# Transposes of the attention weights woven between the projections, values two phases behind their scores, attention weights in two buffers

## The chip, the cores and the metric

The kernel runs on one core of one Trainium2 chip. The metric is the device time in microseconds. TensorE (PE) multiplies matrices and writes PSUM, VectorE (DVE), ScalarE (ACT) and GpSimd (POOL) do the rest, SyncE (SP) issues the DMA transfers. PEld is TensorE's weight load, which has rows of its own.

## What is computed

128 graphs of 128 nodes, model width 512, 16 heads of width 32. All tensors are float32.

```python
q, k, v = (split_heads(x @ W.T) for W in (Wq, Wk, Wv))
a = einsum('bhnd,bhmd->bhnm', q, k) * scale + (adj + adj)[:, None]
a = where(any(a != 0, axis=-1, keepdims=True), a, -inf)
p = softmax(a); p = where(isnan(p), 0, p)
o = merge_heads(einsum('bhnm,bhmd->bhnd', p, v)) @ Wo.T
return layernorm(x + o)
```

## The kernel before, in words

A group is GG = 4 graphs (512 rows of x); there are 32 groups. A group has TILES = 4 phases, one for each four heads, so there are PHASES = 128 phases, numbered f = 4g + t. One phase handles four graphs times four heads, that is 16 score matrices of 128x128.

A projection (kinds k, q, v, o) is one 128x512 product with a contraction over 512. To keep float32 accuracy with the fp32r type, both operands are split in a high and a low part (`split_product`, L334): for each of the four chunks two matmuls (L338 with the low, L339 with the high part crossed) and then four of high times high (L341), 12 matmuls of 128x512 in one PSUM bank. An output of kind k, q or v is copied out of its bank by ACT (`take`, L454), one of kind o is added to x by DVE (`add`, L587), which then takes the statistics for the layernorm; POOL works out the scale and shift (`ln`, L284) and ACT applies them (`normalise`, L486); SP stores.

One phase on PE (L428 to L447) is, in this order:

- `turn(f-1)`, L388: 16 transposes of the last phase's attention weights `e_sb` (128x128 each), four (a quad, one graph) to one bank; ACT copies each quad to `e_t` (`turned_out`, L504).
- `scores(f)`, L397: 16 products, one for each graph and head, that use 32 rows of the array each (the trace has 32 records of them) into four banks `ps_s`.
- `values(f-1)`, L411: the product of `e_t` and v, again 16 products and 32 records, 32 columns of the array each, into `ps_o`. ACT takes the high part (`values_hi`), DVE the low part (`values_lo`).
- the projections of `slots(f)`, four in an inner phase by `PLAN` (L37): k and q for the next head tile, and two of kind v (for the next group) or o (for the last group).

Projections and quads share the BANKS = 3 banks `ps_w` in the order of `bank_uses()` (L72): use u takes bank u mod 3, and `wait_bank(u)` (L344) makes PE wait until use u-3 has been copied out (`k_copied`, `q_copied`, `v_copied`, `turned_copied`, or `added` for o).

DVE's phase: `add` of the last phase's last o, `values_lo(f-2)`, doubling of the adjacency once a group, `bias(f)` (L606, score plus bias and its row minimum, 16 instructions), `any_nonzero` (L621), then in two halves reciprocals (L637) and `normalise` (L645, which multiplies `e_sb`), then `add` of the third slot. ACT's phase: the last copy, the four quads, layernorm, the four `exps(f, i)` (L495, 4 activations each) with the copies of the first two slots among them, `values_hi(f-1)`, layernorm, and one or two splits of x chunks (`chunk_hi`). ACT, DVE, POOL and SP each run their queue strictly in the order written. SP's order of loads and stores is written out in L241 to L260.

The first phase has eight projections (`FIRST_PHASE`); the last group has its own plan (`LAST_PLAN`), and after it the last four o projections follow (`AFTER`). The last group's x is loaded by `load_x(GROUPS - 1)` (L257) into the one buffer `x_sb`, after all stores of the group before it.

Of the kernel before, what the change touches and what calls it, by code (L numbers as in the profile page):

```python
# [8 lines left out]
ACT = mybir.ActivationFunctionType  # L9
# [27 lines left out]
PLAN = [[("k", 1, 0), ("q", 1, 0), ("v", 0, 1), ("v", 1, 1)],  # L37
# [3 lines left out]
FIRST_PHASE = [("k", 1, 0), ("q", 1, 0), ("v", 0, 0), ("v", 1, 0), ("v", 2, 0), ("v", 3, 0), ("v", 0, 1), ("v", 1, 1)]  # L41
# [29 lines left out]

def bank_uses():  # L72

    uses = list(slots(-1))
    for f in range(PHASES + 1):
        if f:
            uses += [("t", f - 1, i) for i in range(GG)]
        uses += slots(f)
    return uses
# [23 lines left out]
def build(nc, xt_d, x_d, adj_d, wq_d, wk_d, wv_d, wo_d, out_d):  # L103
    ctx = ExitStack()
    with ctx:
# [20 lines left out]
        e_sb = sb("e_sb", [P, GG, TH, NODES])  # L126
# [63 lines left out]
        w_stage = {"k": v_sb[:, 1], "q": e_sb[:, :].rearrange("p a b c -> p a (b c)"),  # L190
# [7 lines left out]
        def _(sp):  # L198
# [42 lines left out]
            for g in range(GROUPS):  # L241
                store(g - 2, 3)
                if g + 1 < GROUPS:
                    if g:
                        sp.wait_ge(biased, GG * TILES * g)
                    sp.dma_start(adj_sb[:, (g + 1) % PAIR], adj_d[g + 1]).then_inc(adj_loaded[(g + 1) % PAIR], 16)
                if g:
                    load_x(g - 1)
                load_chunk(g + 2, 0)
                load_chunk(g + 2, 1)  # L250
                store(g - 1, 0)
                store(g - 1, 1)
                load_chunk(g + 2, 2)
                store(g - 1, 2)
                load_chunk(g + 2, 3)
# [7 lines left out]
        def _(pool):  # L263
# [58 lines left out]
            for f in range(PHASES):  # L322
                if f:
                    ln(f - 1, -1)
                chunk_lo(window_chunk(f))
                chunk_lo(late_chunk(f))
                ln(f, -2)
            ln(PHASES - 1, -1)
# [4 lines left out]
        def _(pe):  # L333
# [54 lines left out]
            def turn(f):  # L388
                for i in range(GG):
                    u = USE["t", f, i]  # L390
                    wait_bank(u)
                    pe.wait_ge(normalised, count("t", f, i))
                    for h in range(TH):
                        last = pe.transpose(ps_w[u % BANKS][:, h * P:(h + 1) * P], e_sb[:, i, h, :], ident[:, :])  # L394
                    last.then_inc(turned, 1)
# [32 lines left out]
            for f in range(PHASES + 1):  # L428
                if f:
                    turn(f - 1)  # L430
                if f < PHASES:
                    scores(f)
                if f:
                    values(f - 1)
                for kind, g, index in slots(f):
# [14 lines left out]
        def _(act):  # L450
# [3 lines left out]
            def take(f, s):  # L454

                todo = slots(f)
                if not -len(todo) <= s < len(todo) or todo[s][0] == "o":
                    return
                kind, g, index = todo[s]
                in_ = ps_w[USE[kind, g, index] % BANKS][:, :]  # L460
                act.wait_ge(made[kind], count(kind, g, index))
# [33 lines left out]
            def exps(f, i):  # L495
                if f:
                    act.wait_ge(turned, count("t", f - 1, i))
                act.wait_ge(biased, count("t", f, i))
                for h in range(TH):
                    last = act.activation(e_sb[:, i, h, :], neg_a[:, i, h, :], ACT.Exp, scale=-1.0,  # L500
                                          bias=neg_max[:, i, h:h + 1], accum_out=sums[:, i, h:h + 1])
                last.then_inc(exp_done, 1)

            def turned_out(f):  # L504
                for i in range(GG):
                    if f:
# [215 lines left out]
```

## Time and profile before

| | |
|---|---|
| median of 3 runs | 1979.76 us (1978.6 to 1979.77) |
| the profiled execution | 1979.87 us, its span 1977.9 us |
| PE busy | 1943.8 us (98%), 16384 matmuls |
| ACT busy | 1491.0 us (75%) |
| DVE busy | 1476.5 us (75%) |
| POOL busy | 421.0 us (21%) |
| 16 DMA engines | 17% |
| mean granted TensorE clock | 0.996 of 2.4 GHz |

The largest groups of instructions are the projections' matmuls on PE, the exponentials on ACT (L500, 2048 activations, 792.4 us) and the bias on DVE (L615, 2048 instructions, 442.6 us). A row of the timeline has start and busy time in us, then engine, line, operation, output<-inputs, shapes and count, and in brackets the idle time before it and who ended it. A matmul's busy time is longer than its step: matmuls are pipelined, and the step from one start to the next is what one costs.

### The profile page before, as it was taken

How to read it: one execution, taken by the hardware profiler on the slowest of the kernel's cores; microseconds unless marked ns; L12 is line 12 of the kernel's file. 1: busy time of each engine (PE TensorE's matmuls, PEld its weight loads, DVE VectorE, ACT ScalarE, POOL GpSimd, SP SyncE). 2: the span in 40 equal slices, each digit the busy share in tenths (PEclk: the TensorE clock that was granted, in tenths of full speed). 3: DMA queues.
4: the chain of work that ended last, by engine and by line, in shares of the span. 5: the costliest groups of instructions: out<-in, count | busy, mean ns of one | idle time of the engine just before them, and what ended most of it. 6: DMA issues, size and time to landing. Idle time of an engine off the chain costs nothing. (4 is left out here: it accounts for less than half of the span.)

```text
span 1977.9 us, 49324 instructions
## 1 busy us (share of the span) xinstructions
PE 1943.8 (98%) x16384; PEld 1604.8 (81%) x16384; DVE 1476.5 (75%) x6064; ACT 1491.0 (75%) x5393; POOL 421.0 (21%) x1291
## 2 busy tenths in 40 slices
PE   8999999999999999999999999999999999999995
PEld 6788888888888888888888888888888888888884
DVE  4778777877777787778777778877787777778775
ACT  6877778777777777777777777777777777777783
POOL 2122121222112221212221122212122211222103
PEclk9999999999999999999999999999999999999998
DMA  4120112211122101122111222011221111220101
GB/s 149 49 70 29 55 60 71 70 39 55 54 65 70 69 30 54 60 70 71 38 55 54 65 71 71 28 54 60 70 70 38 55 55 65 71 70 29 44 33 65
DMA packets 48637, 116.41 MB, mean 59 GB/s; under 512 B 5376, under 2 KB 5376, under 8 KB 44288
## 3 DMA queue, kind: packets, MB, share of 16 engines
q1 hardware_dynamic: 48384, 113.27, 17.0%
q8 instruction: 131, 2.15, 0.5%
q14 instruction: 122, 1.00, 0.2%
HBM read 79.69 MB, written 33.55 MB: 57 GB/s over the span
## 5 line engine op out<-in xcount | busy, mean ns | idle before, releaser
L500 ACT ACTIVATE e_sb<-neg_a,neg_max 128x128 f32<-128x128 f32 x2048 | 792.4, 389 | 110.2 <-DVE neg_max L615 110.2
L615 DVE CUSTOM_DVE_ANT_0 neg_a<-ps_s,adj_sb 128x128 f32<-128x128 f32 x2048 | 442.6, 286 | 353.9 <-PE ps_s L407 353.9
L338 PE MATMUL ps_w<-xt_hi,w_lo 128*128 128x512 f32 x1024 | 415.8, 406 | 9.0 <-DVE w_lo L569 7.1
L452 ACT ACTIVATE e_t<-ps_w 128x512 f32<-128x512 f32 x512 | 267.1, 599 | 204.8 <-PE ps_w L394 203.5
L339 PE MATMUL ps_w<-xt_lo,w_hi 128*128 128x512 f32 x1024 | 401.2, 392 | 0.0
L500 ACT ACTIVATION_READ_ACCUMULATOR e_sb<-neg_a,neg_max 128x1 f32 x2048 | 385.3, 188 | 0.0
L656 DVE SCALAR_TENSOR_TENSOR e_sb<-e_sb,r_inv 128x512 f32<-128x512 f32 x512 | 332.3, 690 | 9.2 <-DVE r_inv L652 0.5
L623 DVE TENSOR_REDUCE neg_min<-neg_a 128x16 f32<-128x2048 f32 x128 | 292.6, 2286 | 4.4
L276 POOL TENSOR_TENSOR xt_lo<-xt_raw,xt_hi 128x512 fp32r<-128x512 f32 x120 | 155.2, 1294 | 628.6 <-ACT xt_hi L452 628.6
L341 PE MATMUL ps_w<-xt_hi,w_hi 128*128 128x512 f32 x1024 | 274.9, 390 | 0.0
L394 PE MATMUL ps_w<-ident,e_sb 128*128 128x128 f32 x2048 | 262.4, 278 | 11.0 <-DVE x_sb L598 6.1
L394 PEld LDWEIGHTS ps_w<-ident,e_sb 128*128 128x128 f32 x2048 | 228.5, 140 | 48.8 <-DVE x_sb L598 7.0
L338 PEld LDWEIGHTS ps_w<-xt_hi,w_lo 128*128 128x128 f32 x1024 | 192.4, 188 | 73.5 <-issue 32.4
L341 PEld LDWEIGHTS ps_w<-xt_hi,w_hi 128*128 128x128 f32 x1024 | 192.8, 188 | 41.3
L339 PEld LDWEIGHTS ps_w<-xt_lo,w_hi 128*128 128x128 f32 x1024 | 193.0, 188 | 36.6
L299 POOL TENSOR_TENSOR ln_tmp<-mean_var,constants 128x1 f32<-128x1 f32 x128 | 25.0, 196 | 838.0 <-DVE mean_var L604 831.9
L338 PE MATMUL ps_w<-w_hi,o_lo 128*128 128x512 f32 x512 | 199.8, 390 | 1.5 <-DVE o_lo L569 1.5
L339 PE MATMUL ps_w<-w_lo,o_hi 128*128 128x512 f32 x512 | 199.2, 389 | 0.0
L338 PE MATMUL ps_w<-w_hi,xt_lo 128*128 128x512 f32 x512 | 199.2, 389 | 0.0
L339 PE MATMUL ps_w<-w_lo,xt_hi 128*128 128x512 f32 x512 | 199.2, 389 | 0.0
L452 ACT ACTIVATE v_sb<-ps_w 128x512 f32<-128x512 f32 x128 | 76.3, 596 | 142.7 <-PE ps_w L341 142.6
L615 DVE DVE_READ_ACCUMULATOR2_ANT neg_max<- 128x1 f32 x2048 | 170.3, 83 | 0.0
(56 smaller groups left out, 2495.8 us busy)
## 6 DMA issues: line engine op xcount, KB each, us to landing
x_sb<-x SPq DMA_DIRECT2D x32, 1024.0 KB, 4.9
out<-x_sb SPq DMA_DIRECT2D x128, 256.0 KB, 2.5
xt_raw<-xt SPq DMA_DIRECT2D x120, 256.0 KB, 2.9
adj_sb<-adj SPq DMA_DIRECT2D x32, 256.0 KB, 3.0
neg_a<-xt SPq DMA_DIRECT2D x4, 256.0 KB, 5.5
v_sb<-wk SPq DMA_DIRECT2D x4, 256.0 KB, 6.4
e_sb<-wq SPq DMA_DIRECT2D x4, 256.0 KB, 7.1
v_sb<-wv SPq DMA_DIRECT2D x4, 256.0 KB, 7.8
```

The lines of the kernel that those rows point to most:

```text
L276: return pool.tensor_tensor(out, whole, hi.bitcast(F32), ALU.subtract)
L299: pool.tensor_tensor(ve, mean_var[:, i, 1:2], eps, ALU.add).then_inc(pool_step, 1)
L338: pe.matmul(out, lhs_lo(c), rhs_hi(c), start=(c == 0), stop=False)
L339: pe.matmul(out, lhs_hi(c), rhs_lo(c), start=False, stop=False)
L341: last = pe.matmul(out, lhs_hi(c), rhs_hi(c), start=False, stop=(c == chunks - 1))
L394: last = pe.transpose(ps_w[u % BANKS][:, h * P:(h + 1) * P], e_sb[:, i, h, :], ident[:, :])
L452: return act.activation(out, in_, ACT.Copy, scale=scale)
L500: last = act.activation(e_sb[:, i, h, :], neg_a[:, i, h, :], ACT.Exp, scale=-1.0, bias=neg_max[:, i, h:h + 1], accum_out=sums[:, i, h:h + 1])
L615: last = dve.tensor_tensor_reduce(out=neg_a[:, i, h, :], in0=ps_s[h][:, i * NODES:(i + 1) * NODES], in1=adj_sb[:, g % PAIR, i, :], scale=- ...
L623: dve.tensor_reduce(neg_min[:, :].rearrange("p a b -> p (a b)"), neg_a[:, :].rearrange("p a b c -> p (a b) c"), AX.X, ALU.max).then_inc(mi ...
L656: dve.scalar_tensor_tensor(out=e_sb[:, i], in0=e_sb[:, i], scalar=BIG, in1=r_inv[:, i].unsqueeze(2).to_broadcast([P, TH, NODES]), op0=ALU. ...
```

## The change

- PE: `woven(f)` puts the quads of phase f-1 between the projections of phase f, one behind each of the four (with fewer projections, two quads may stand together). Scores of f come first, `values(f-2)` directly behind them, then the woven list.
- `e_sb` has two buffers (by phase parity), since the weights of phase f-1 are still read when the exponentials of phase f are written. `w_stage["q"]` moves with it.
- ACT: copies follow the woven order (two uses behind `exps` 1, two behind `exps` 2, two behind `exps` 3, the last two at the start of the next phase); `values_hi(f-2)` now stands ahead of the exponentials.
- DVE: `values_lo(f-2)` moves from before `bias` to behind it.
- Plan: v of the own group's graphs 2 and 3 in t = 0, v of the next group's graphs 0 and 1 in t = 1, o in t = 2 and t = 3. The first phase has six projections, the last group 4, 3, 2 and 3.
- SP: the two chunk loads stand ahead of the stores, and the third store of a group moves to the next group's turn.

The diff, cut to its core:

```diff
-PLAN = [[("k", 1, 0), ("q", 1, 0), ("v", 0, 1), ("v", 1, 1)],
-        [("k", 2, 0), ("q", 2, 0), ("o", 0, -1), ("o", 1, -1)],
-        [("k", 3, 0), ("q", 3, 0), ("o", 2, -1), ("o", 3, -1)],
-        [("k", 0, 1), ("q", 0, 1), ("v", 2, 1), ("v", 3, 1)]]
-LAST_PLAN = [[("k", 1, 0), ("q", 1, 0), ("k", 2, 0)],
-             [("q", 2, 0), ("k", 3, 0), ("q", 3, 0)],
-             [("o", 0, -1), ("o", 1, -1)],
-             [("o", 2, -1), ("o", 3, -1)]]
+PLAN = [[("k", 1, 0), ("q", 1, 0), ("v", 2, 0), ("v", 3, 0)],
+        [("k", 2, 0), ("q", 2, 0), ("v", 0, 1), ("v", 1, 1)],
+        [("k", 3, 0), ("q", 3, 0), ("o", 0, -1), ("o", 1, -1)],
+        [("k", 0, 1), ("q", 0, 1), ("o", 2, -1), ("o", 3, -1)]]
+FIRST_PHASE = [("k", 1, 0), ("q", 1, 0), ("v", 0, 0), ("v", 1, 0), ("v", 2, 0), ("v", 3, 0)]
+LAST_PLAN = [[("k", 1, 0), ("q", 1, 0), ("v", 2, 0), ("v", 3, 0)],
+             [("k", 2, 0), ("q", 2, 0), ("k", 3, 0)],
+             [("q", 3, 0), ("o", 0, -1)],
+             [("o", 1, -1), ("o", 2, -1), ("o", 3, -1)]]
...
+def woven(f):
+
+    todo = slots(f)
+    if f <= 0 or f == PHASES:
+        return ([("t", f - 1, i) for i in range(GG)] if f > 0 else []) + todo
+    uses = []
+    for s, use in enumerate(todo):
+        uses.append(use)
+        uses += [("t", f - 1, i) for i in range(GG) if i * len(todo) // GG == s]
+    return uses
...
-        e_sb = sb("e_sb", [P, GG, TH, NODES])
+        e_sb = sb("e_sb", [P, PAIR, GG, TH, NODES])
...
             for g in range(GROUPS):
-                store(g - 2, 3)
...
+                load_chunk(g + 2, 0)
+                load_chunk(g + 2, 1)
+                store(g - 2, 2)
+                store(g - 2, 3)
                 if g:
                     load_x(g - 1)
-                load_chunk(g + 2, 0)
-                load_chunk(g + 2, 1)
+                load_chunk(g + 2, 2)
                 store(g - 1, 0)
+                load_chunk(g + 2, 3)
                 store(g - 1, 1)
...
             for f in range(PHASES + 1):
-                if f:
-                    turn(f - 1)
                 if f < PHASES:
                     scores(f)
-                if f:
-                    values(f - 1)
-                for kind, g, index in slots(f):
+                if f > 1:
+                    values(f - 2)
+                for use in woven(f):
+                    kind, g, index = use
+                    if kind == "t":
+                        turn(g, index)
+                        continue
+                    if f == PHASES and index == 0:
+                        values(PHASES - 1)
...
             for f in range(PHASES):
+                for use in woven(f - 1)[6:]:
+                    take(use)
+                if f > 1:
+                    values_hi(f - 2)
+                if f == 1:
+                    act.wait_ge(w_lo_done, 2 * CH)
+                exps(f, 0)
+                exps(f, 1)
+                uses = woven(f)
+                for use in uses[0:2]:
+                    take(use)
+                if f and f != PHASES - 1:
+                    normalise(f - 1, -2)
+                exps(f, 2)
+                for use in uses[2:4]:
+                    take(use)
+                chunk_hi(window_chunk(f))
+                exps(f, 3)
+                if f == 0:
+                    weight_hi("o")
+                for use in uses[4:6]:
+                    take(use)
                 if f:
...
                     normalise(f - 1, -1)
                 chunk_hi(late_chunk(f))
...
             for f in range(PHASES):
-                if f:
+                if f and f != PHASES - 1:
                     add(f - 1, -1)
-                if f > 1:
-                    values_lo(f - 2)
                 if f % TILES == TILES - 1 and f + 1 < PHASES:
                     double_adj(f // TILES + 1)
                 bias(f)
+                if f == PHASES - 1:
+                    add(f, 0)
+                if f > 1:
+                    values_lo(f - 2)
                 any_nonzero(f)
+                if f == PHASES - 1:
+                    add(f, 1)
                 reciprocals(f, 0)
                 abs_largest(f)
                 normalise(f, 0)
                 reciprocals(f, 1)
                 normalise(f, 1)
-                add(f, -2)
-            add(PHASES - 1, -1)
+                if f == PHASES - 2:
+                    add(f, 1)
+                elif f != PHASES - 1:
+                    add(f, -2)
             values_lo(PHASES - 2)
+            add(PHASES - 1, 2)
             values_lo(PHASES - 1)
```

## Rows read from the trace of the kernel before

**Rows 1.** Stretches cut at the scores of phases 4 and 124: busy time, clock
```profile
0.00:83.15 83.15, 69.60 (x504) 54.63 (x505) 51.21 (x193) 60.55 (x192) 15.10 (x22) 1.00 0.33 115
83.15:1896.12 1812.97, 1812.67 (x15361) 1500.98 (x15361) 1373.52 (x5670) 1383.86 (x5038) 389.88 (x1197) 1.00 0.17 57
1896.12:1977.90 81.78, 61.55 (x521) 49.17 (x520) 51.81 (x201) 46.58 (x165) 15.97 (x72) 0.89 0.13 51
```

**Rows 2.** Timeline of PE, an inner phase (f = 54, t = 2) and the next transposes
```profile
838.69 1.17 PE L407 MATMUL ps_s<-k_sb,q_sb 32*128 32x128 f32 x32
...
840.81 0.50 PE L338 MATMUL ps_w<-xt_hi,w_lo 128*128 128x512 f32 x1
841.14 0.39 PE L339 MATMUL ps_w<-xt_lo,w_hi 128*128 128x512 f32 x1
...
843.66 0.39 PE L338 MATMUL ps_w<-xt_hi,w_lo 128*128 128x512 f32 x1
...
846.38 0.39 PE L338 MATMUL ps_w<-w_hi,o_lo 128*128 128x512 f32 x1
...
851.83 2.04 PE L394 MATMUL ps_w<-ident,e_sb 128*128 128x128 f32 x16
```

**Rows 3.** The same view just before it, cut to the first four of its sixteen transposes
```profile
836.73 0.60 PE L394 MATMUL ps_w<-ident,e_sb 128*128 128x128 f32 x4
```

**Rows 4.** The page, section 5: the group of the transposes' matmuls
```profile
L394 PE MATMUL ps_w<-ident,e_sb 128*128 128x128 f32 x2048 | 262.4, 278 | 11.0 <-DVE x_sb L598 6.1
```

**Rows 5.** Weight loads (PEld) and matmuls where projections end and transposes begin
```profile
821.43 0.58 PEld L394 LDWEIGHTS ps_w<-ident,e_sb 128*128 128x128 f32 x4
...
821.66 2.00 PE L394 MATMUL ps_w<-ident,e_sb 128*128 128x128 f32 x16
```

**Rows 6.** Timeline of DVE in that phase
```profile
839.93 0.29 DVE L615 CUSTOM_DVE_ANT_0 neg_a<-ps_s,adj_sb 128x128 f32<-128x128 f32 x1 [0.80 <-PE ps_s L407]
...
843.43 2.29 DVE L623 TENSOR_REDUCE neg_min<-neg_a 128x16 f32<-128x2048 f32 x1
...
847.83 0.20 DVE L643 RECIPROCAL recip<-sums 128x8 f32<-128x8 f32 x1
...
849.53 0.68 DVE L598 TENSOR_TENSOR x_sb<-ps_w,x_sb 128x512 f32<-128x512 f32 x1
...
852.03 0.69 DVE L598 TENSOR_TENSOR x_sb<-ps_w,x_sb 128x512 f32<-128x512 f32 x1 [0.87 <-PE ps_w L341]
...
853.58 0.66 DVE L569 TENSOR_TENSOR o_lo<-ps_o,o_hi 128x512 fp32r<-128x512 f32 x1
854.15 0.44 DVE L579 TENSOR_SCALAR adj_sb<-adj_sb 128x512 f32<-128x512 f32 x1
```

**Rows 7.** Timeline of ACT in that phase
```profile
840.96 0.40 ACT L500 ACTIVATE e_sb<-neg_a,neg_max 128x128 f32<-128x128 f32 x1 [0.75 <-DVE neg_max L615]
...
844.06 0.58 ACT L452 ACTIVATE k_sb<-ps_w 128x512 f32<-128x512 f32 x1
...
848.58 0.81 ACT L492 ACTIVATE x_sb<-x_sb,shift,rstd 128x512 f32<-128x512 f32 x1
849.28 0.62 ACT L452 ACTIVATE xt_hi<-xt_raw 128x512 fp32r<-128x512 f32 x1
```

**Rows 8.** Timeline of PE: the scores of phase 0
```profile
18.79 1.17 PE L407 MATMUL ps_s<-k_sb,q_sb 32*128 32x128 f32 x32 [0.78 <-ACT q_sb L452]
```

**Rows 9.** Timeline of the tail, PE, then DVE
```profile
1932.43 0.66 PE L394 MATMUL ps_w<-ident,e_sb 128*128 128x128 f32 x4 [2.19 <-DVE x_sb L598]
1933.95 1.97 PE L394 MATMUL ps_w<-ident,e_sb 128*128 128x128 f32 x8 [0.87 <-DVE x_sb L598]
...
1962.41 0.69 DVE L598 TENSOR_TENSOR x_sb<-ps_w,x_sb 128x512 f32<-128x512 f32 x1 [7.61 <-DMA x_sb<-x]
```

**Rows 10.** The chain of work that ended last: store and load before the last adds
```profile
1955.25 2.38 DMA out<-x_sb
1957.64 4.75 DMA x_sb<-x
```

More of the change, by code:

```diff
@@ L69, in count @@
     return GG * g + index + 1
-def bank_uses():
-    uses = list(slots(-1))
-    for f in range(PHASES + 1):
-        if f:
-            uses += [("t", f - 1, i) for i in range(GG)]
-        uses += slots(f)
-    return uses
+def woven(f):
[7 more added lines that the diff above has]
+    return uses
+def bank_uses():
+    return [use for f in range(-1, PHASES + 1) for use in woven(f)]
 USES = bank_uses()
@@ L326, in _ @@
                 chunk_lo(late_chunk(f))
-                ln(f, -2)
-            ln(PHASES - 1, -1)
+                if f == PHASES - 1:
+                    ln(f, 0)
+                    ln(f, 1)
+                elif f == PHASES - 2:
+                    ln(f, 1)
+                else:
+                    ln(f, -2)
+            ln(PHASES - 1, 2)
             for s in range(GG):
@@ L386, in first_product, with turn @@
                 weight_product(kind, 0, index, before if index == 0 else None)
[L388 to L395, printed above, removed]
+            def turn(f, i):
+                u = USE["t", f, i]
+                wait_bank(u)
+                pe.wait_ge(normalised, count("t", f, i))
+                for h in range(TH):
+                    last = pe.transpose(ps_w[u % BANKS][:, h * P:(h + 1) * P], e_sb[:, f % PAIR, i, h, :], ident[:, :])
+                last.then_inc(turned, 1)
             def scores(f):
@@ L452, in copy, with take @@
                 return act.activation(out, in_, ACT.Copy, scale=scale)
-            def take(f, s):
-                todo = slots(f)
-                if not -len(todo) <= s < len(todo) or todo[s][0] == "o":
+            def take(use):
+                kind, g, index = use
+                if kind == "o":
                     return
-                kind, g, index = todo[s]
-                in_ = ps_w[USE[kind, g, index] % BANKS][:, :]
-                act.wait_ge(made[kind], count(kind, g, index))
+                in_ = ps_w[USE[use] % BANKS][:, :]
+                if kind == "t":
+                    if g:
+                        act.wait_ge(values_done, g)
+                    else:
+                        act.wait_ge(xt_lo_done, CH)
+                    act.wait_ge(turned, count(*use))
+                    copy(e_t[:, index].rearrange("p a b -> p (a b)"), in_).then_inc(turned_copied, 1)
+                    return
+                act.wait_ge(made[kind], count(*use))
                 if kind == "v":
@@ L495, in exps @@
             def exps(f, i):
[L496 to L497 removed]
+                if f >= PAIR:
+                    act.wait_ge(turned, count("t", f - PAIR, i))
                 act.wait_ge(biased, count("t", f, i))
                 for h in range(TH):
[L500 removed]
+                    last = act.activation(e_sb[:, f % PAIR, i, h, :], neg_a[:, i, h, :], ACT.Exp, scale=-1.0,
                                           bias=neg_max[:, i, h:h + 1], accum_out=sums[:, i, h:h + 1])
                 last.then_inc(exp_done, 1)
[L504 to L512 removed]
             def values_hi(f):
@@ L526, in _ @@
             weight_hi("q")
[L527 removed]
+            take(("k", 0, 0))
             weight_hi("v")
[L529 removed]
+            take(("q", 0, 0))
             for c in range(CH):
```

51 lines of the change are left out of this document (11 added, 40 removed).

## The prediction

> **What bounds the kernel now.** Read first the busy times by stretch [rows 1]. The trace is cut where the scores of phase 4 and of phase 124 start: a head of 83.15 us, 30 inner groups in 1812.97 us (60.43 us a group), a tail of 81.78 us. In the inner stretch PE is busy 1812.67 of 1812.97 us at a granted clock of 1.00, so nothing can be won there by removing idle time: only a shorter step of the matmuls themselves counts. DVE and ACT are busy 76% of it. In head and tail PE is idle 13.6 and 20.2 us, and in the tail the clock is at 0.89 on average.
>
> Next the steps of one inner phase [rows 2]: scores and values 2.12 us (838.69 to 840.81), the first projection 2.85 us, a further one 2.72 us, the transposes from 836.73 [rows 3] to the scores at 838.69, 1.96 us, the phase 15.10 us (836.73 to 851.83). So 60.40 us a group.
>
> **The transposes, from both sides.** Four take 0.60 us [rows 3], and one takes 0.278 [rows 4], so the step is (0.60 - 0.28) / 3 = 0.109 us. Sixteen without a wait would have 15 x 0.109 + 0.28 = 1.91 us of busy time; they have 2.00 in half of the phases [rows 5] and 2.04 in the others [rows 2]. So 0.10 to 0.13 us a phase are lost inside the block by rounding. Another 0.09 (1.96 less 15 x 0.109, less the lost 0.13, less one step) goes on the change to the 32-row scores. Inside the block it is the third and fourth quad that lose. Their banks were last used by the last projection and by the first quad, which ended 1 us earlier, so their weight loads wait for the copies. Where the bank is free, the first quad's loads start 0.23 us ahead of the matmuls, during the last projection matmul [rows 5].
>
> In the changed kernel a quad and a projection alternate. A use three back ended at least one projection and one quad earlier, 2.72 + 0.44 = 3.2 us, so the bank waits inside the block go. Over the four phases they are worth 0.10 + 0.13 + 0.13 + 0.10 = 0.47 us a group. The last quad still borders on the scores, and scores, values and first projection keep their order, so 2.12, 2.85 and 0.09 stay.
>
> What no row shows is a projection right behind a transpose. Lower bound: nothing, as from projection to transpose [rows 5], since both use the whole array. Upper bound: the price of the projection behind the values, 2.85 against 2.72 [rows 2]; 0.11 of it is the first weight load that is not ahead (0.33 us from the first matmul to the second instead of 0.23), and about 0.03 to 0.04 are slightly long steps in the next six matmuls (0.23, 0.24, 0.23 instead of 0.227). There are three such borders in a full phase, about 375 in all. I take nothing: the nearest row is the other border of the same two shapes, and the loads of a transpose run at the same step as the transposes. The middle case, where the slightly long steps come back at every border, is 375 x 0.04 = 15 us.
>
> That full-array work may follow full-array work without a break agrees with the Trainium skill (TensorEngine Tiling, Key Properties): changing the tiling mode drains TensorE, changing only the tile does not. Another page of the Trainium skill speaks against the change (TensorE: Matmul & The Clock Gate, Part 3, The mechanism): a weight load overlaps with matmuls in flight only when the row group differs. By that each of the new borders would expose a load, as in rival 2 below. The trace does not agree: the loads of the first quad start 0.23 us ahead on the same rows [rows 5].
>
> **The inner stretch: who is late next.** I lay one phase out from the start of its scores (0), with the durations above. PE: values end at 2.1, quads at 5.4, 8.6, 11.7, the fourth projection ends and the fourth quad should start at 14.44, the next scores at 14.98.
>
> ACT, with steps from [rows 7]: four exponentials of one graph 1.55 (two graphs 3.10, 840.96 to 844.06), a layernorm 0.70 (848.58 to 849.28, busy 0.81, so about 0.10 overlaps with the next), a copy 0.48 and a chunk split 0.52 (busy 0.58 and 0.62, less that 0.10). `values_hi` now leads and waits for the values of this phase, 0.09 behind their last start: 2.21. In t = 3, the fullest phase: 2.21 + 0.48 + 3.10 (to 5.79) + two copies 0.97 + layernorm 0.70 + exponentials 1.55 + two copies 0.97 + chunk 0.52 + exponentials 1.55 = 12.05. Copies wait nowhere. The other late wait, the fourth quad's copy, which the values of the next phase need 1.9 us into it, ends at 0.6.
>
> DVE, from [rows 6]: bias 3.50, reduction and first half 4.40 (843.43 to 847.83), second half 1.70, an add 1.55 (852.03 to 853.58) whose first 0.68 frees the bank, low part 0.57, doubling 0.44. In t = 3 it starts with the add of t = 2's last o (to 1.20) and the doubling (1.64), bias to 5.14, low part 5.71, first half 10.1. The second half needs the last sums, which ACT has at 12.05; with 0.15 us for the hand-over (ACT starts at 840.96, four bias steps of 0.22 behind 839.93 [rows 6, 7]) it runs 12.2 to 13.9. Only then comes `add(f, -2)`, and its output bank is the one that the fourth quad needs: free at 14.6, wanted at 14.44 and, for its load, at 14.21. So the fourth quad starts 0.25 us late (0 to 0.8, as the ACT chain is 0.4 us shorter or longer) in one phase of four. In t = 2 ACT has no layernorm and no chunk ahead of the last exponentials, so everything is 1.2 us earlier: no wait. In t = 0 and 1 ACT copies the v at 12.6: no wait. Before, this add had a whole projection more time.
>
> Group: 60.40 - 0.47 + 0.25 = 60.18 us, against 60.43 measured, so 30 x 0.25 = 7.5 us are won.
>
> **Head.** The scores of phase 0 stay at 18.79 [rows 8]. Phase 0: scores 1.10 (busy 1.17 [rows 8]), first projection 2.85, five at 2.72, 0.09: phase 1 starts at 36.4. It has no values: 1.10 + 2.85 + 3 x 2.72 + 1.83 = 13.95, phase 2 at 50.4. Phase 2 has two projections and two quads between them; the second projection needs the first one's bank, which ACT copies only behind the second exponentials (5.8 + 0.5), 0.6 late: 10.15, phase 3 at 60.5. DVE's second half of phase 2 ends at 13.2, which is 3.05 into phase 3: doubling and bias from 3.05, first exponentials at 4.45, k copied behind the second ones at 8.0, its successor in the bank runs 8.2 to 10.9, with two quads 11.9: phase 4 at 72.4. There the last quad's copy comes 2.7 in, so the values end 1.0 late. So 73.4 against 83.15 for the head with two projections fewer (5.44 us), and one block of transposes and one of values fewer.
>
> **Tail.** Phase 124 is full, 14.98. Phase 125: 2.12 + 2.85 + 2 x 2.72 + 1.83 + a wait of 0.6 = 12.9. Phase 126: 2.12 + 2.85 + 2.72 + 1.83 + 0.6 = 10.15. So the scores of 127 start 38.0 us into the tail. There DVE is behind: its 126 ends 3.6 us into 127, bias to 7.1, so the second projection, whose bank the first add frees, waits from 5.85 to 8.0; the values of 126 run at 14.5 to 15.6; the second quad of 127 waits for the last add, which comes behind both halves and a low part (17.5 to 18.2). Idle spells of that length halve the clock in the tail of before: after 2.19 and 0.87 us idle, eight transposes take 1.97 us [rows 9] where eight steps are 0.87. The last two quads and the values, about as many steps, make 1.8 us. Then the last layernorm of group 30 starts at 23.9 (it stands behind `values_hi(127)` on ACT), 0.82 later the store, 2.38 and 4.75 us for store and load [rows 10], and from the first add the 15.5 us of before (1962.41 [rows 9] to 1977.90) to the end: 47.4. Tail 38.0 + 47.4 = 85.4 against 81.78, though it holds 8.4 us more of PE work.
>
> **Sum.** Head 73.4 + groups 1805.4 (30 x 60.18) + tail 85.4 = 1964.2 us of span, plus 1.97 around it (1979.87 - 1977.9) = 1966.2. The median of the runs of before, 1979.76, is within 0.1 us of the profiled one. I predict 1966 us, -0.7%.
>
> SP's new order costs nothing: the load of x is issued about 2 us into t = 1 and lands 5 us later, its first add is at 11 us of t = 2; chunk loads are issued at least 4 us ahead of their splits. The second buffer of `e_sb` costs no time.
>
> **Rivals.**
> 1. Long steps behind every quad (the middle case): 1966 + 15 = 1981, no change. For it: each projection in the trace that starts without a load ahead has them. Against: here the load is ahead by one transpose. Chance 0.35.
> 2. Each return to a projection costs the full 0.13 to 0.16 us, load and long steps: 375 x 0.15 = 56 us, 2022, slower. From (14 + 4) / 375 = 0.05 us a border on the kernel is slower. For it: a projection has never stood directly behind a small matmul with a load ahead. Against: [rows 5]. With the next one, 0.15 in all. The rule of the Trainium skill on row groups (TensorE: Matmul & The Clock Gate, Part 3) would give this rival.
> 3. The late add: if ACT's chain is 0.6 us longer, every t = 3 waits 0.9 and t = 2 starts to wait: 30 x 0.9 = 27 us more, 1993, slower; if it is shorter, 30 x 0.25 = 7.5 less, 1959.
> 4. That the weaving saves nothing in the block (the waits were something else, such as the clock): 1966 + 14 = 1980, within rival 1.
>
> **How the numbers follow.** Forecast 0.5 (1956 to 1975), rival 1 0.35, rivals 2 and 3 upward 0.15. Low 1955: no late add and a warm tail. High 1988: rival 1 with 0.06 us a border. About 0.2 is left out, mostly above. A measurement tells 0.2% (4 us) from no change. Faster (under 1975.8): 0.47 + 0.10 from rival 1's short end = 0.57. Same 0.20. Slower 0.23.
>
> **What would show it.** In the timeline of PE after: quads of 0.44 us between projections of 2.72 us (rivals 1 and 2: 2.76, 2.87); a wait of the fourth quad for the add (`x_sb`) of about 0.25 us in t = 3 alone; phase 4 at 72 to 73 us; the second half of the tail with one clock drop. The prediction is wrong if ACT is idle for longer than its values wait in an inner phase, if the weight loads of a projection behind a quad do not start with the last transpose, or if a group takes over 60.5 us.

## The result and the profile after

The changed kernel takes 1985.41 us (median of 8 runs, 1982.71 to 1986.39) against 1979.59 us of the kernel before on the same chip (8 runs, 1978.41 to 1979.95): a ratio of 1.0029, 95% interval 1.0018 to 1.004. It is slower by 0.3%, where 1966 us was forecast. The profiled execution is 1983.31 us, its span 1981.4 us; it is one of the shorter ones, so the traces show 3.4 us of the 5.8 us between the medians.

| | before | after |
|---|---|---|
| head, to the scores of phase 4 | 83.15 us | 73.62 us |
| 30 inner groups | 1812.97 us | 1823.36 us |
| tail, from the scores of phase 124 | 81.78 us | 84.42 us |
| PE busy | 1943.8 us | 1949.9 us |
| DVE busy, ACT busy | 1476.5, 1491.0 us | 1471.2, 1494.5 us |

Busy time by stretch after, cut at the same scores. As in [rows 1] the columns are the stretch, its length, the busy time of PE, PEld, DVE, ACT and POOL, the clock, and the DMA share and rate:

```profile
0.00:73.62 73.62, 60.90 (x433) 47.52 (x433) 50.03 (x188) 54.10 (x175) 13.39 (x20) 1.00 0.30 104
73.62:1896.98 1823.36, 1822.64 (x15362) 1485.36 (x15361) 1367.38 (x5672) 1389.85 (x5046) 395.09 (x1181) 1.00 0.18 57
1896.98:1981.40 84.42, 66.37 (x593) 52.86 (x592) 53.75 (x205) 50.54 (x173) 21.07 (x90) 0.95 0.16 57
```

The loss is all in the inner stretch. PE works there without idle time at a granted clock of 1.00, as it did before, and takes 10.4 us longer for the same matmuls: the steps themselves have become longer. Head and tail together gave 6.9 us back (158.0 against 164.9). A steady group takes 60.75 us, against 60.40 before and 60.18 forecast; its phases t = 0 to 3 take 15.12, 15.14, 15.14 and 15.35 us (medians over the 30 groups, from the starts of the scores).

PE's timeline in phase 56 (t = 0) of after, from one quad to the next:

```profile
869.41 0.60 PE L406 MATMUL ps_w<-ident,e_sb 128*128 128x128 f32 x4
869.77 0.48 PE L351 MATMUL ps_w<-xt_hi,w_lo 128*128 128x512 f32 x1
870.08 0.40 PE L352 MATMUL ps_w<-xt_lo,w_hi 128*128 128x512 f32 x1
870.32 0.40 PE L351 MATMUL ps_w<-xt_hi,w_lo 128*128 128x512 f32 x1
870.55 0.40 PE L352 MATMUL ps_w<-xt_lo,w_hi 128*128 128x512 f32 x1
870.79 0.39 PE L351 MATMUL ps_w<-xt_hi,w_lo 128*128 128x512 f32 x1
...
871.71 1.08 PE L354 MATMUL ps_w<-xt_hi,w_hi 128*128 128x512 f32 x4
872.62 0.60 PE L406 MATMUL ps_w<-ident,e_sb 128*128 128x128 f32 x4
```

A quad and the projection behind it take 3.21 us (869.41 to 872.62), where 2.72 + 4 x 0.109 = 3.156 was forecast. The records' starts, to the nanosecond, give the steps of that projection as 315, 235, 233, 236, 224, 231, 236, 228, 232, 231, 227, 230 ns (from one start to the next); a projection behind a projection has 226 or 227 throughout. I call the steps above 227 the long steps, and the place where a projection follows a transpose a border or a return. The first, 315, is hardly an addition of its own: the last transpose of the quad takes only 28 ns to the next start instead of 109, so the pair has 343 for 336. What is lost is in the next nine steps.

The weight loads of the same place:

```profile
869.18 0.58 PEld L406 LDWEIGHTS ps_w<-ident,e_sb 128*128 128x128 f32 x4
869.74 0.19 PEld L351 LDWEIGHTS ps_w<-xt_hi,w_lo 128*128 128x128 f32 x1
869.85 0.19 PEld L352 LDWEIGHTS ps_w<-xt_lo,w_hi 128*128 128x128 f32 x1
```

The projection's first load starts with the last transpose (869.74), as the forecast asked for, and still the long steps are there.

### The profile page after: what moved, and what is told of

It is laid out like the page before. It is cut to its first block and busy times, and to the rows that moved or that the text cites. A ratio compares the mean times of both kernels' runs of the same rounds, so it can differ in the third digit from the quotient of the medians.

```text
span 1981.4 us, 49320 instructions
## 1 busy us (share of the span) xinstructions
PE 1949.9 (98%) x16384; PEld 1585.7 (80%) x16384; DVE 1471.2 (74%) x6064; ACT 1494.5 (75%) x5393; POOL 429.5 (22%) x1291
## 5 line engine op out<-in xcount | busy, mean ns | idle before, releaser
L351 PE MATMUL ps_w<-xt_hi,w_lo 128*128 128x512 f32 x1024 | 428.2, 418 | 12.2 <-DVE w_lo L586 8.3
L468 ACT ACTIVATE e_t<-ps_w 128x512 f32<-128x512 f32 x512 | 302.0, 591 | 146.5 <-PE ps_w L406 146.1
L523 ACT ACTIVATION_READ_ACCUMULATOR e_sb<-neg_a,neg_max 128x1 f32 x2048 | 394.8, 193 | 0.0
L406 PEld LDWEIGHTS ps_w<-ident,e_sb 128*128 128x128 f32 x2048 | 250.8, 139 | 74.9 <-DVE x_sb L615 14.0
L406 PE MATMUL ps_w<-ident,e_sb 128*128 128x128 f32 x2048 | 306.2, 272 | 1.8 <-DVE x_sb L615 1.8
L660 DVE RECIPROCAL recip<-sums 128x8 f32<-128x8 f32 x256 | 50.7, 198 | 233.9 <-ACT e_sb L523 233.9
L468 ACT ACTIVATE o_hi<-ps_o 128x512 fp32r<-128x512 f32 x128 | 76.7, 599 | 192.6 <-PE ps_o L433 192.5
L351 PE MATMUL ps_w<-w_hi,o_lo 128*128 128x512 f32 x512 | 212.3, 415 | 4.0 <-DVE x_sb L615 1.9
L351 PE MATMUL ps_w<-w_hi,xt_lo 128*128 128x512 f32 x512 | 212.0, 414 | 0.0
```

The source lines that it names most:

```text
L351: pe.matmul(out, lhs_lo(c), rhs_hi(c), start=(c == 0), stop=False)
L468: return act.activation(out, in_, ACT.Copy, scale=scale)
L523: last = act.activation(e_sb[:, f % PAIR, i, h, :], neg_a[:, i, h, :], ACT.Exp, scale=-1.0, bias=neg_max[:, i, h:h + 1], accum_out=sums[:, ...
L660: dve.reciprocal(recip[:, two], sums[:, two]).then_inc(recip_done, 1)
```

## The experiments

All are edits of the changed kernel. A group's or a phase's time is the median over the 30 inner groups, read from the starts of the scores.

**More and fewer borders.** If every return from a transpose to a projection costs the same, the number of returns sets the time. The first kernel cuts three quads of a full phase in two and puts the second half ahead of the last four matmuls of the next projection (the two `held` lines stand in `split_product`): six returns instead of three.

```diff
-                for h in range(TH):
-                    last = pe.transpose(...)
-                last.then_inc(turned, 1)
...
+                while held:
+                    held.pop(0)()
...
+                some((0, 1))
+                if len(slots(f + 1)) == 4 and i < GG - 1 and f + 1 < PHASES:
+                    held.append(lambda: some((2, 3)))
+                else:
+                    some((2, 3))
```

> The changed kernel, but the quads behind the first three projections of a full phase are cut in two: two transposes behind the projection, two in the middle of the next projection (ahead of its four high times high matmuls). A full phase has six places where a projection's matmul follows a transpose, not three. Theory A, each return from a transpose to a projection matmul costs about 0.05 us, whatever bank or semaphore stands there: a phase goes from 15.14 to 15.29 us, 125 x 0.15 = 19 us slower than the changed kernel, about 2004 us. Theory B, the price belongs to the start of a projection (new bank, bank wait): no change, 1985 us, and no long steps behind the inner pair.

Measured: 2050.91 us, ratio 1.0361 (1.0346 to 1.0377), far from either number, but for another reason than the returns:

```profile
893.97 0.66 PE L412 MATMUL ps_w<-ident,e_sb 128*128 128x128 f32 x4 [1.16 <-DVE x_sb L629]
...
899.53 0.38 PE L412 MATMUL ps_w<-ident,e_sb 128*128 128x128 f32 x2
899.66 0.48 PE L353 MATMUL ps_w<-xt_hi,w_lo 128*128 128x512 f32 x1
...
901.60 0.38 PE L412 MATMUL ps_w<-ident,e_sb 128*128 128x128 f32 x2
901.73 1.17 PE L358 MATMUL ps_w<-xt_hi,w_hi 128*128 128x512 f32 x4
902.74 0.38 PE L412 MATMUL ps_w<-ident,e_sb 128*128 128x128 f32 x2
```

The second half of a quad ends 2 us later, so its copy on ACT and the exponentials behind it come later (DVE's second half waits 403.2 us for them over the run, against 233.9 in after), at last the late `add` too, and the fourth quad waits for the bank: t = 2 takes 16.05 and t = 3 16.52 us. The line at 893.97 is such a wait, in t = 3. That is the prediction's rival 3, at another size. Where no quad waits the returns can be read: t = 0 takes 15.14 and t = 1 15.17 us, against 15.12 and 15.14 with half the returns. A quad and its projection take 3.21 us in both kernels (899.53 to 902.74). So a return has no fixed price. Each begins a series of long steps, and the second return cuts off the first one's series; with few matmuls behind it, it is cheap. The expectation that each return costs 0.05 us falls.

The second kernel takes one border out. ACT's copies follow the new order: those of the projections stay in the same gaps between the exponentials, those of the second and third quad move one gap later.

```diff
+FULL = ['p0', 't0', 'p1', 'p2', 't1', 'p3', 't2', 't3']
+CUTS = (2, 3, 5)
...
+    if len(todo) == 4:
+        return [("t", f - 1, int(w[1])) if w[0] == "t" else todo[int(w[1])] for w in FULL]
```

> The changed kernel with the full phases in the order P0 T0 P1 P2 T1 P3 T2 T3 (ACT's copies follow it). Each use still has at least one projection and one quad between it and its bank's last use, but a projection follows a quad twice, not three times. Theory A (price per return): 0.05 us a phase less, a group from 60.75 to 60.55, 6 us less in all, about 1979 us. Theory B: if the price is the slow steps' own (the clock, contention with ACT or DVE), the projections behind projections keep them and the time stays at 1985.

Measured: 1979.03 us, ratio 0.9999 (0.999 to 1.0009); a group takes 60.53 to 60.56 us. The projection behind a projection is back at 2.72 us. Taking out one border of three wins 6.4 us by the medians (30 x 0.22 = 6.6 by the groups), about what the change had lost (5.8).

The third takes them all out. The quads stand in one block behind the fourth projection (`FULL` = p0 to p3, then t0 to t3):

> The changed kernel with the four quads in a block behind the fourth projection in full phases, scores and values as in the changed kernel. Theory A: no projection follows a quad, so projections two to four take 2.72 us each; in t = 0 and 1 the phase falls from 15.14 to about 15.07 (0.15 less for the borders, 0.1 more for the banks of the third and fourth quad). In t = 2 and 3 the third quad waits about 0.4 and 1.3 us for the add of the fourth o, which now comes late on DVE: 15.4 and 16.3. In all about 1993. Theory B: projections two to four keep 2.77 even without a quad before them.

Measured: 2043.34 us, a single run. Phases t = 0 and 1 take 15.07 us, near the 15.10 of before: without borders there are no long steps, and the third and fourth quad again wait for the copies of their banks, 0.04 and 0.06 us by their steps. That is 0.05 to 0.07 less than with three borders (15.12 and 15.14), so the weaving loses more than it saves even where no add is late. In t = 2 and 3 it is worse, since three banks are all there are:

```profile
873.25 1.21 PE L416 MATMUL ps_w<-ident,e_sb 128*128 128x128 f32 x8
875.32 1.09 PE L416 MATMUL ps_w<-ident,e_sb 128*128 128x128 f32 x8 [0.86 <-DVE x_sb L625]
```

The third quad needs the bank of the fourth projection, an o, whose add stands behind the second half of the weights on DVE. Each of these phases takes 16.2 to 16.4 us; the third quad's wait was expected, but in size for t = 3 alone. (The phases that the expectation names add up to 61.84 us a group, about 2018 us in all and not its 1993.) So with these plans and three banks a block behind the projections is no way back: woven, only one quad in sixteen waits for the add.

**The late add by itself.** In t = 3 of after the chain is the one laid out in the prediction, nearly to the tenth. Its rows on DVE, then PEld:

```profile
922.16 0.20 DVE L660 RECIPROCAL recip<-sums 128x8 f32<-128x8 f32 x1 [2.34 <-ACT e_sb L523]
922.45 0.17 DVE L669 SCALAR_TENSOR_TENSOR r_inv<-recip,nonzero 128x8 f32<-128x8 f32 x1
922.65 1.29 DVE L673 SCALAR_TENSOR_TENSOR e_sb<-e_sb,r_inv 128x512 f32<-128x512 f32 x2
923.86 0.68 DVE L615 TENSOR_TENSOR x_sb<-ps_w,x_sb 128x512 f32<-128x512 f32 x1
...
924.60 0.42 PEld L406 LDWEIGHTS ps_w<-ident,e_sb 128*128 128x128 f32 x4 [0.42 <-DVE x_sb L615]
```

The scores of that phase start at 909.84, so the second half starts 12.3 us into it (forecast 12.2) and the bank is free at 14.7 (forecast 14.6). Over the run the fourth quad's load waits 30 times:

```profile
PEld ps_w L406 <- DVE x_sb L615: 14.0, 30, 2.0
```

The edit puts the add ahead of the second half of the weights, into DVE's 2.34 us of waiting:

```diff
                 normalise(f, 0)
+                if f < PHASES - 2:
+                    add(f, -2)
                 reciprocals(f, 1)
                 normalise(f, 1)
                 if f == PHASES - 2:
                     add(f, 1)
-                elif f != PHASES - 1:
-                    add(f, -2)
```

> The changed kernel with DVE's add of the third slot's o moved ahead of the second half of the reciprocals. Theory: in t = 3 the fourth quad waits 0.21 us because that add comes last on DVE; with it ahead, in DVE's idle time, t = 3 falls from 15.35 to 15.14, 31 x 0.21 = 6.5 us less, about 1979 us. Rival: the wait is for another copy, and t = 3 keeps 15.35.

Measured: 1980.45 us (1974.7 to 1981.41), ratio 1.0 (0.999 to 1.001). The wait is gone: all phases take 15.10 us and a group 60.40 instead of 60.75, the group of before. Only 0.25 us of it are in t = 3; the other three phases are 0.02 to 0.04 us shorter, since the series of long steps are shorter there behind the values (2.863 us for 2.881, except in t = 0) and behind the first quad (2.835 for 2.857). PE's program is the same in both kernels, so how long a series gets is not set by the matmuls ahead alone; what sets it no run shows. 30 x 0.35 = 10.5 us are won in the inner groups, and the profiled execution (1976.35 us) is 7.0 us faster than the changed kernel's. Its head takes 76.93 instead of 73.62 us. 1.75 us of that lie ahead of the scores of phase 0, where the edit changes nothing: they start at 20.07 instead of 18.32 us, and over the twelve kernels that have a trace here they start anywhere from 18.1 to 20.1. The other 1.56 us are in phase 3. Both kernels have an idle spell of 2.7 us on PE there; here it is followed by a stretch at half clock (matmuls of 512 columns step by 0.43 us), in after it is not. Two stretches of the head by clock, of this kernel and then of after:

```profile
72.00:76.00 4.00, 4.00 (x13) 3.03 (x12) 2.92 (x7) 1.95 (x9) 0.00 (x0) 0.57 0.00 0
```

```profile
72.00:76.00 4.00, 3.36 (x60) 2.62 (x58) 1.72 (x5) 3.35 (x13) 1.27 (x1) 1.00 0.01 4
```

The runs of this kernel lie 6.7 us apart, and their mean clocks between 0.995 and 0.997. Phase 3 takes 14.7 to 14.8 us in seven of the nine kernels that share its order, and 13.2 in after and in one other, and in those seven matmuls of 512 columns step by 0.43 us for a while; the profiled execution of after was a lucky one. The start and this drop together make up to 3.5 us; the rest of the 6.7 stays open.

**What makes the steps long?** The trace leaves two causes. Either the load of the projection's weights is ahead by too little (0.03 us, 869.74 to 869.77, against 0.23 inside a projection, 869.85 to 870.08), because a transpose is so short, or the steps follow a change from fp32 matmuls (the transposes) to fp32r ones. The first test makes the matmul ahead long: one fp32 product of 512 columns in place of the four transposes.

```diff
-                for h in range(TH):
-                    last = pe.transpose(ps_w[...][:, h * P:(h + 1) * P], e_sb[:, f % PAIR, i, h, :], ident[:, :])
+                last = pe.matmul(ps_w[...][:, :], ident[:, :], e_sb[:, f % PAIR, i].rearrange(...), start=True, stop=True)
```

> The changed kernel with each quad of transposes replaced by one product of the identity with the quad's 512 columns (float32, two passes of 512 columns). It leaves out the transposition, so its output is not the reference's. Question: what makes the steps behind a quad long. Theory C, a weight load that has only one short matmul (0.109 us) of lead when the projection begins: behind a long matmul the load is fully ahead, the steps are 0.227 at once and the projections behind a quad take 2.72 us. Theory D, the change of type from fp32 to fp32r: the long steps stay and they take about 2.78. The product itself is longer than four transposes (about 0.86 against 0.44 us), so the whole takes about 200 us more.

Measured: 2185.37 us, a single run (the product is longer than the quad; this says nothing here). PE, then PEld:

```profile
862.25 1.02 PE L405 MATMUL ps_w<-e_sb,ident 128*128 128x512 f32 x2
862.71 0.80 PE L351 MATMUL ps_w<-w_hi,o_lo 128*128 128x512 f32 x1
863.35 0.40 PE L352 MATMUL ps_w<-w_lo,o_hi 128*128 128x512 f32 x1
863.58 0.40 PE L351 MATMUL ps_w<-w_hi,o_lo 128*128 128x512 f32 x1
...
862.68 0.19 PEld L351 LDWEIGHTS ps_w<-w_hi,o_lo 128*128 128x128 f32 x1 [0.24 <-issue]
863.11 0.19 PEld L352 LDWEIGHTS ps_w<-w_lo,o_hi 128*128 128x128 f32 x1 [0.24 <-issue]
```

The first load ends at 862.87, and the second load, which elsewhere starts about 0.1 us or less behind the start of its forerunner's matmul (869.85 against 869.77 in after), starts at 863.11: the first matmul streams from about there, with its weights loaded 0.24 us before. The steps behind it are still 233, 236, 224, 231, 236, 228, 233, 231 ns. A short lead is not the cause; it was not needed for long steps here.

The second test keeps four short matmuls of the same shape, but of type fp32r (weights times weights, with nothing read from the attention weights; the waits for semaphores ahead of them stay):

```diff
-                    last = pe.transpose(ps_w[...], e_sb[:, f % PAIR, i, h, :], ident[:, :])
+                    cols = slice(h * P, (h + 1) * P)
+                    last = pe.matmul(ps_w[...], w_hi[:, 1, h, cols], w_hi[:, 0, h, cols], start=True, stop=True)
```

> The changed kernel with the four transposes of a quad replaced by four fp32r products of 128 columns between parts of the weights. It leaves out the transposition and does not read the attention weights, so its output is not the reference's. Theory C (short matmul, short lead): long steps behind each quad as in the changed kernel, T and P together 0.04 to 0.06 us over the sum of their own steps. Theory D (change of type): no long steps, projections of 2.72 us.

Measured: 1973.04 us, a single run.

```profile
865.87 0.56 PE L407 MATMUL ps_w<-w_hi 128*128 128x128 f32 x4
866.26 0.45 PE L351 MATMUL ps_w<-xt_hi,w_lo 128*128 128x512 f32 x1
866.55 0.40 PE L352 MATMUL ps_w<-xt_lo,w_hi 128*128 128x512 f32 x1
866.78 0.39 PE L351 MATMUL ps_w<-xt_hi,w_lo 128*128 128x512 f32 x1
...
869.05 0.56 PE L407 MATMUL ps_w<-w_hi 128*128 128x128 f32 x4
```

A quad with its projection takes 3.18 us. The steps are 283, 232, 231, 227, 227: the series has two long ones instead of nine. Neither theory had that: it is 0.024 us above the 3.156 that theory D expected, of which 0.013 are the quad's own steps (112 ns for 109) and 0.010 the two long ones. But here the quads do not read the attention weights, so the next kernel has the quads in place: the attention weights times an identity of type fp32r.

```diff
-        e_sb = sb("e_sb", [P, PAIR, GG, TH, NODES])
+        e_sb = sb("e_sb", [P, PAIR, GG, TH, NODES], F32R)
+        q_stage = sb("q_stage", [P, GG, TH * NODES])
...
+        ident_r = sb("ident_r", [P, P], F32R)
...
+            pool.tensor_tensor(ident_r[:, :], ident[:, :], ident[:, :], ALU.mult).then_inc(consts, 1)
...
-                    last = pe.transpose(ps_w[...], e_sb[:, f % PAIR, i, h, :], ident[:, :])
+                    last = pe.matmul(ps_w[...], e_sb[:, f % PAIR, i, h, :], ident_r[:, :], start=True, stop=True)
```

> The changed kernel whose quads stay in place and still read the attention weights, but as fp32r products with an identity of type fp32r in place of fp32 transposes (the attention weights are rounded to fp32r on the way). Theory D (the long steps behind a quad come from the change of type from fp32 to fp32r): as with the short fp32r quads, a quad with its projection takes 3.18 instead of 3.21 us, phases t = 0 to 2 15.03 instead of 15.12 to 15.14, t = 3 15.26, a group 60.38 instead of 60.75, so 11 us less than the changed kernel: 1974 us. Rival E (the gain of the short fp32r quads came from not reading the attention weights, that is, from waits on the exponentials and products that fell away): a quad with its projection stays at 3.21, the group at 60.75, the time at 1985 us.

Measured: 1974.3 us (1973.55 to 1974.75, 7 runs), ratio 0.9969 (0.9957 to 0.998).

```profile
873.39 0.56 PE L410 MATMUL ps_w<-ident_r,e_sb 128*128 128x128 f32 x4
873.78 0.45 PE L355 MATMUL ps_w<-w_hi,xt_lo 128*128 128x512 f32 x1
874.07 0.40 PE L356 MATMUL ps_w<-w_lo,xt_hi 128*128 128x512 f32 x1
...
876.57 0.56 PE L410 MATMUL ps_w<-ident_r,e_sb 128*128 128x128 f32 x4
```

3.18 us again (873.39 to 876.57), phases t = 0 to 2 at 14.99, 0.13 to 0.15 below those of after, the group 60.33, the time where the type theory had it. About half of that is at the three returns (0.03, 0.016 and 0.03 us); the rest is in the last quad ahead of the scores (0.488 for 0.528) and in the projection behind the values (2.852 for 2.881). Only t = 3 stays at 15.35: there the add sets the fourth quad's start, and cheaper matmuls ahead of it turn into waiting. Seven or so of the nine long steps behind a quad are a matter of the type of the matmul ahead: both fp32 kinds, transposes and the long product, bring the long series, and both fp32r kinds bring two steps. It is not the only way to get them. In the trace of before a projection in the tail follows matmuls of type fp32r, and its first load is late behind a wait (PE, then PEld):

```profile
1962.24 1.07 PE L341 MATMUL ps_w<-w_hi,o_hi 128*128 128x512 f32 x4
1963.16 0.50 PE L338 MATMUL ps_w<-w_hi,o_lo 128*128 128x512 f32 x1
1963.16 0.19 PEld L338 LDWEIGHTS ps_w<-w_hi,o_lo 128*128 128x128 f32 x1 [0.27 <-DVE x_sb L598]
```

Its steps are 337, 236, 228, 233, 231, 226.

**The repairs together.** Two borders and the early add:

> Both repairs of the inner phase at once: order P0 T0 P1 P2 T1 P3 T2 T3 and DVE's add ahead of the second half. Theory: both add up in the profile, a group from 60.75 to 60.3 (four phases of 15.07), 14 us less than the changed kernel in an undisturbed run: 1971 to 1975, about 0.3% faster than the kernel before. Rival: the copies of the changed order come late on ACT once the DVE wait is gone, and the group stays at 60.4 or more.

Measured: 1973.59 us, ratio 0.9965 (0.9953 to 0.9978), a group 60.32 us, as the theory had it. Three more edits work on head and tail: phases with two or three projections, except phase 126, have their quads as p0 t0 p1 t1 and then the rest; in the last phase the add of the third o stands ahead of the second half of the weights; and ACT's first layernorm of the last phase stands ahead of its last copy of the values.

> The same, and the short phases at both ends in an order in which no projection needs the bank of the projection just before it (P0 T0 P1 T1 and so on), the last o of the group before last added ahead of the second half of its phase, and its layernorms on ACT ahead of the last copy of the values. Theory: the waits of the first and last phases (0.6 us in phase 125, up to 2.9 us in phase 3, about 1.2 us ahead of the last store) shrink: 3 to 4 us less than two_borders_add_early, 1968 to 1971. Rival: the ends are bound by DVE's and ACT's own length of 12 to 13 us a phase, and nothing moves.

Measured: 1967.86 us (1967.62 to 1968.8, 5 runs), ratio 0.994 (0.9927 to 0.9954): faster than the kernel before and the changed one, with the same arithmetic. It is 5.7 us less than with the inner repairs alone, where 3 to 4 were expected. In the traces, which lie 6.0 us apart, 0.7 us are in phase 2, 2.3 in phase 3, 2.3 in the tail, and 0.8 ahead of the scores of phase 0, which no edit touches. And with the fp32r quads, which round the attention weights to fp32r:

> The kernel with two borders a phase, the earlier add and the rearranged head and tail, with the quads as fp32r products as well. Theory D: eight returns a group at 0.03 us less each, a group 60.08 instead of 60.32 us, 7 us less than the 1967.9 us of the same kernel with transposes: 1961 us. Rival E: 60.32 us a group and 1968 us, as with transposes.

Measured: 1957.02 us (1956.22 to 1959.36, 4 runs), ratio 0.9884 (0.987 to 0.9899). The windows of these last two, cut at the scores of phases 4 and 124, first with transposes and then with fp32r quads:

```profile
72.84:1883.58 1810.74, 1810.00 (x15361) 1492.81 (x15361) 1394.92 (x5675) 1390.59 (x5046) 432.89 (x1187) 1.00 0.18 57
1883.58:1965.70 82.12, 65.78 (x593) 52.88 (x592) 53.14 (x204) 50.76 (x174) 19.66 (x84) 0.96 0.16 59
```

```profile
71.82:1870.99 1799.17, 1799.17 (x15362) 1521.20 (x15361) 1391.04 (x5673) 1389.10 (x5046) 431.69 (x1187) 1.00 0.18 58
1870.99:1954.40 83.41, 68.87 (x593) 56.89 (x592) 53.37 (x205) 50.79 (x174) 19.64 (x85) 0.91 0.16 58
```

A group takes 59.92 us, 0.40 less than with transposes; 0.24 was expected, 0.03 for each of eight returns. By the steps each phase wins 0.10: 0.031 and 0.016 at the two returns, 0.023 in the first projection, whose series behind the values is shorter too (2.852 us for 2.875), and 0.030 in the two quads that stand together ahead of the scores (0.934 for 0.964). The last two I had not counted. No phase waits for an add here, so nothing is lost again.

## Why the prediction was wrong, point by point

**The step that failed** is the price of a projection behind a transpose: "I take nothing: the nearest row is the other border of the same two shapes". Measured are 0.055, 0.040 and 0.055 us for the three borders of a phase, 0.15 a phase and 0.60 a group, 18 us over the 30 inner groups. The forecast for these was 1805.4 us and they took 1823.4 (1.1 of that is the late copy of phase 4, which the forecast had counted in the head). The term was mis-sized, and the other terms of the inner group are almost right. The middle case, rival 1, was the true one: long steps behind every quad, at 0.05 instead of 0.04 us a border, because the series behind a quad lasts up to nine steps and not six. The prediction said that from 0.05 us a border on the kernel is slower, and so it came out, by a hair. Its own sign of being wrong, a group over 60.5 us, is there (60.75).

The reason was in the argument and not in the trace. Rows 5 show a transpose behind a projection, and I took it as a row for the opposite order. The row that belonged there was the projection behind the values [rows 2], whose small steps (0.23, 0.24, 0.23) I had seen and laid to the load that was not ahead. Two things were together in that row, a late load and a matmul of type fp32 ahead. The borders of after show the second without the first, and the projection at 1963.16 in the tail of before the first without the second: either alone brings long steps.

**Rival 2** (load and long steps, 0.15 us a border) falls: the load is hidden. **The rule on row groups** of the Trainium skill (TensorE: Matmul & The Clock Gate, Part 3, The mechanism), by which a weight load overlaps with matmuls only on other row groups, is not borne out at the new border either: the projection's load starts at 869.74, as the last transpose starts, on all rows. The same section of the Trainium skill excepts loads into the background weight buffer, which the prediction left out.

**The bank waits inside the block** did go. A quad has its steps of 0.109 us and no more, in each of the four places but the one in t = 3. The transposes took 1.93 to 1.97 us a phase before, 7.80 a group, and without the borders they take 7.34, so the weaving won 0.46 us a group, about the 0.47 that was worked out, and rival 4, that it saves nothing there, falls. The long steps took that and 0.14 more.

**The late add** was right: forecast 0.25 us in t = 3 alone, measured 0.21 (15.35 against 15.14). The size owes something to chance, since the prediction's own 14.6 and 14.44 differ by 0.16. **Rival 3** did not come in this kernel. The run with halved quads shows how near it was: with copies that are later on ACT t = 2 starts to wait as well, and it costs 2.1 us a group (62.88 against 60.75).

The first projections, behind the values, hardly changed: 2.86 to 2.88 us now and 2.85 to 2.89 before, 0.02 us more a group. (The 2.85 of [rows 2] is one of the shorter ones, and the 60.40 of before already holds them all.) Added up for a group: 60.18 + 0.60 for the borders + 0.02 for the first projections - 0.04 for the add = 60.76, against 60.75 measured. One division of the prediction is off, (0.60 - 0.28) / 3, which is 0.107; the 0.109 that it goes on with is what the records have (108 or 109 ns), so nothing hangs on it.

**Head and tail** were right in sum. The scores of phases 1 to 4 were forecast at 36.4, 50.4, 60.5 and 72.4 us and came at 35.97, 50.07, 60.40 and 73.62 (the first 0.47 us of that is an earlier start of phase 0, which is chance); phase 4 has the forecast late copy (16.25 us long). The miss at phase 4 is the wait for the bank in phase 3, in the place foreseen, 1.2 us longer. The tail took 84.42 against 85.4. Of its waits for an add in phase 127, which starts at 1935.70, the second and third are close to where they were laid out (7.7 and 18.0 us into the phase, forecast 8.0 and about 18.2); the first, 0.45 us, was not foreseen:

```profile
1938.34 0.50 PE L351 MATMUL ps_w<-w_hi,o_lo 128*128 128x512 f32 x1 [0.45 <-DVE x_sb L615]
1943.39 0.50 PE L351 MATMUL ps_w<-w_hi,o_lo 128*128 128x512 f32 x1 [1.16 <-DVE x_sb L615]
...
1953.66 1.53 PE L406 MATMUL ps_w<-ident,e_sb 128*128 128x128 f32 x12 [1.81 <-DVE x_sb L615]
```

The forecast clock drop is not in this execution: twelve transposes behind 1.81 us of idle time take 1.53 us, at full clock, where eight took 1.97 behind 2.19 and 0.87 us in [rows 9]. The 0.95 of the tail comes from its last 10 us, where PE has nothing left to do. That the sum of head and tail came out right is in part luck: without this drop the tail was short of the forecast by 1.0 us, and the head over it by 1.2. Five of the eight runs are 1.8 to 3.1 us longer than the profiled one, at a mean clock of 0.997 instead of 0.998; a later start and a drop in phase 3, as in add_early, would be of that size, but these runs have no trace.

**The range** held the time, at its upper end. The chances leaned too far to faster: a case whose price sat at the point of decision had 0.35.

## What to carry to other kernels

Where a full engine is the bound, count its returns from one kind of matmul to another before you weave them: here a return from fp32 to fp32r matmuls cost 0.04 to 0.055 us, which took back all that the weaving won; with fp32r quads it cost 0.024. A border is priced by a row of the same order, not of its reverse. And an operation that frees a buffer belongs into its engine's idle time ahead of the work that waits, not behind that work: moving one add won 0.35 us a group, 0.25 of it in the phase that had waited, and taking out a border 0.22.

## What the runs showed of the hardware

- Behind fp32 transposes, fp32r matmuls of 128x512 step by 228 to 236 ns (one by 224) for five to nine steps and then by 226.7 ns; behind short fp32r matmuls there are two such steps (232, 231), and behind a late load with fp32r ahead four. Nearly all series are pieces of one pattern, 235 233 236 224 231 236 228 233 231 226 227, entered at another place. What the engine catches up in these steps, and what sets the place, no run shows.
- An interruption inside a series hardly adds to it: six returns in a phase cost 0.015 to 0.033 us more than three.
- The steady step, 226.7 ns for 512 columns at a granted clock of 1.00 with a weight load between all matmuls, is above the 215.7 ns that the Trainium skill gives for back-to-back matmuls of that size (TensorE: Matmul & The Clock Gate, Part 1, Wait — 56ns, not 53.3ns?). No run here leaves the loads out, so whether they are the difference stays open.
- An idle spell of 2.7 us on PE in the head was followed by a stretch at half clock in add_early and not in after, with the same work on PE around it (0.57 and 1.00 above, steps of 0.43 and 0.23 us).
